# Gated delta attention on one core: the gate's projection is copied to SBUF, and the orders on ScalarE and VectorE change

## The reference, cut to what matters

```python
x = x + 0.5 * ffn(layernorm(x))
x = x + attention(layernorm(x))        # this part
...
# attention, for every head; chunks of 64 rows in the reference
q, k = l2norm(x @ Wq) / 4, l2norm(x @ Wk)
v, gate = x @ Wv, x @ Wg
P = strict_lower(k_beta @ k.T * L)
Ainv = (I + P) * (I + P^2) * (I + P^4) ...
v, k_cumdecay = Ainv @ (v * beta), Ainv @ (k_beta * exp(g))
# scan over the chunks with a state S per head
v_new = v - k_cumdecay @ S
o = q * exp(g) @ S + tril(q @ k.T * L) @ v_new
S = S * exp(g_last) + (k * exp(g_last - g)).T @ v_new
o = rmsnorm(o) * norm_w
o = o * silu(gate)                     # gate * sigmoid(gate)
x = x + o @ Wo
```

## Time and profile before

| what | value |
|---|---|
| median of 3 executions | 1187.23 us (1185.53 to 1190.21) |
| the profiled execution's own time | 1186.16 us |
| its span, first to last instruction | 1184.0 us |
| VectorE busy over the span | 927.2 us, 78% |
| TensorE matmuls busy over the span | 1005.2 us, 85% |
| ScalarE, GpSimd busy over the span | 604.0 us (51%), 408.4 us (34%) |
| mean granted TensorE clock | 0.942 of full speed |

### The profile page before, as it was taken

How to read it: one execution, slowest core, us unless ns; L and a number is a source line. 1 busy time by engine, 2 the same in 40 slices (tenths; PEclk the granted TensorE clock), 3 DMA queues, 4 the chain that set the end, 5 groups by cost and what they waited for, 6 DMA issues and landing times. The chain is left out here.

```text
span 1184.0 us, 38519 instructions
## 1 busy us (share of the span) xinstructions
PE 1005.2 (85%) x15510; PEld 721.5 (61%) x15510; DVE 927.2 (78%) x2432; ACT 604.0 (51%) x1614; POOL 408.4 (34%) x580
## 2 busy tenths in 40 slices
PE   2999977686898989989888887679999896799967
PEld 1888873354555555555565556558888774255546
DVE  3777646349999999999999999527776456899976
ACT  2433326444677777777777775654333262201144
POOL 2667540301221222222222221216665458500047
PEclk9999999788899999999999988879999888899989
DMA  9100005244544445444455543200000023945003
GB/s 251 32 2 1 1 1 174 55 89 100 110 97 107 105 94 110 103 84 105 105 111 111 111 93 76 44 2 1 2 1 1 11 65 87 282 116 170 1 19 125
DMA packets 282626, 93.31 MB, mean 79 GB/s; under 512 B 208977, under 2 KB 275409, under 8 KB 282449
## 3 DMA queue, kind: packets, MB, share of 16 engines
q1 hardware_dynamic: 247056, 84.03, 29.6%
q10 hardware_dynamic: 35392, 6.82, 3.0%
HBM read 56.20 MB, written 30.41 MB: 73 GB/s over the span
## 5 line engine op out<-in xcount | busy, mean ns | idle before, releaser
L1770 DVE TENSOR_TENSOR delta_tmp<-delta_PR 128x130 f32<-128x130 f32 (+12 forms) x416 | 156.4, 376 | 8.9
L1767 DVE TENSOR_TENSOR delta_PR<-delta_PR,delta_tmp 128x130 f32<-128x130 f32 (+12 forms) x416 | 152.5, 367 | 9.3
L1882 POOL TENSOR_TENSOR delta_S<-delta_E,delta_Bm 128x128 f32<-128x128 f32 x32 | 16.9, 527 | 265.3 <-issue 227.4
L1620 ACT ACTIVATE delta_y<-psum 32x128 f32<-32x128 f32 x256 | 68.7, 268 | 60.4 <-PE psum L1455 57.8
L506 POOL TENSOR_TENSOR ffn_H<-ffn_hid,ffn_H 128x512 fp32r<-128x512 f32 x48 | 61.8, 1293 | 57.0 <-DVE ffn_H L472 57.0
L506 POOL TENSOR_TENSOR first_H<-first_hid,first_H 128x512 fp32r<-128x512 f32 x48 | 61.7, 1290 | 52.9 <-DVE first_H L472 52.9
L1636 ACT ACTIVATE delta_wide<-delta_S 32x128 f32<-32x128 f32 x256 | 78.2, 306 | 3.2
L1405 PE MATMUL psum<-delta_MV,delta_KT 32*32 32x128 f32 x2048 | 66.2, 280 | 10.9 <-ACT delta_E L1570 10.9
L438 ACT ACTIVATE first_silu<-psum 128x512 f32<-128x512 f32 x48 | 28.8, 599 | 83.3 <-PE psum L391 83.3
L1421 PE MATMUL psum<-delta_T,delta_pad 128*32 128x128 f32 x2048 | 70.4, 295 | 0.9 <-issue 0.9
L1858 POOL TENSOR_TENSOR delta_VK<-delta_QK,both_eg 128x256 f32<-128x256 f32 x32 | 20.9, 655 | 145.4 <-DVE delta_QK L1703 145.3
(11 more groups left out here) (278 smaller groups left out, 2541.7 us busy)
## 6 DMA issues: line engine op xcount, KB each, us to landing
within_scratch<-delta_PT SPq DMA_DIRECT2D x128, 64.0 KB, 2.0
delta_PR<-within_scratch SPq DMA_DIRECT2D x16, 512.0 KB, 3.8
inverse_scratch<-delta_PR SPq DMA_DIRECT2D x16, 512.0 KB, 3.1
space_T<-taps_scratch SPq DMA_DIRECT2D x8, 1024.0 KB, 5.9
X<-taps_scratch SPq DMA_DIRECT2D x8, 1024.0 KB, 9.0
X<-in_x SPq DMA_DIRECT2D x32, 128.0 KB, 10.1
turned_scratch<-gates_XT SPq DMA_DIRECT2D x16, 256.0 KB, 2.3
delta_xT<-turned_scratch SPq DMA_DIRECT2D x32, 128.0 KB, 2.9
```

Source lines behind the costliest of these rows:

```text
L1620: i = a.activation(dst, heads(bank[6][rows, half * P:(half + 1) * P]), ACT.Copy)
L1767: i = v.tensor_tensor(after, after, t3, ALU.add)
L1770: i = v.tensor_tensor(t3, column.to_broadcast([P, j, n_after]), row.to_broadcast([P, j, n_after]), ALU.mult)
```

## The change

There are four edits, all in the delta phase.

1. A new SBUF tile `raw_gate`. ScalarE's new step `keep_g` does the first exp of the sigmoid and then copies the gate's projection from PSUM to `raw_gate`; before the copy it waits for `keep_gate` of the tile before (`p_gate`), which reads the same buffer.
2. `p_v` is now signalled by that copy, not by `keep_v`. TensorE's `outputs` waits for `p_v` where it waited for `p_gate`, and so does `project_vg` in the first tiles.
3. On ScalarE the second `widen` stands between `keep_g` and the rest of the sigmoid (ln, exp).
4. On VectorE `keep_gate` reads `raw_gate` in place of PSUM and stands behind turn 17 of the solver, not behind turn 12.

```diff
+    M.raw_gate = take("raw_g", DM)
...
         elif t > 0:
-            pe.wait_ge(S.p_gate, t)
+            pe.wait_ge(S.p_v, t)
...
     def outputs(t):
         if t + LAG_SCAN < NT:
-            pe.wait_ge(S.p_gate, t + LAG_SCAN + 1)
+            pe.wait_ge(S.p_v, t + LAG_SCAN + 1)
...
-        a.activation(of_heads(M.VK[t % 6], 0), heads(bank[5][:, 0:DM]), ACT.Copy).then_inc(S.p_v, 1)
+        a.activation(of_heads(M.VK[t % 6], 0), heads(bank[5][:, 0:DM]), ACT.Copy)
...
-    def sigmoid_g(t):
+    def keep_g(t):
         gate = M.gate[t % 9]
         a.wait_ge(S.p_vg, t + 1)
         if t >= 9:
             a.wait_ge(S.o_gate, t - 8)
         own.seq(a.activation(gate, bank[5][:, DM:], ACT.Exp, scale=-1.0))
+        if t > 0:
+            a.wait_ge(S.p_gate, t)
+        a.activation(M.raw_gate, bank[5][:, DM:], ACT.Copy).then_inc(S.p_v, 1)
+
+    def sigmoid_g(t):
+        gate = M.gate[t % 9]
         own.seq(a.activation(gate, gate, ACT.Ln, bias=1.0))
         a.activation(gate, gate, ACT.Exp, scale=-1.0).then_inc(S.p_sig, 1)
...
         at(keep_v, n)
+        at(keep_g, n)
+        at(widen, Z, 1)
         at(sigmoid_g, n)
-        at(widen, Z, 1)
         at(exp_decays, n - LAG_FORM)
...
-        v.tensor_tensor(gate, gate, bank[5][:, DM:], ALU.mult).then_inc(S.p_gate, 1)
+        v.tensor_tensor(gate, gate, M.raw_gate, ALU.mult).then_inc(S.p_gate, 1)
...
-        solve(n, 12, 13)
+        solve(n, 12, 18)
         at(keep_gate, n)
-        solve(n, 13, 21)
+        solve(n, 18, 21)
```

## The result

The changed kernel takes 1192.13 us (median of 15; 1187.83 to 1199.4), the kernel before 1187.05 (15; 1183.97 to 1194.98). The ratio is 1.004, 95% interval 1.0022 to 1.0058: slower by 0.4%, which is within the 0.5% that the prediction called no change, though the interval lies above 1 as a whole. The forecast was 1188.5, so the range held the time and the middle was low by 3.6.

The account below looks back on a forecast made before the run. The prediction took VectorE's instructions to bound the delta phase from 285 to 753 us. Its terms, -2.8 + 2.7 + 0.3 + 0.8 + 0.3 = +1.3 us, on 1187.23 gave 1188.5 us, range 1184.0 to 1193.0.

Parts of the forecast that it names:

- two rivals: Delta phase: turn blocked for its whole fading overlap, 1191.7, 10 in 100; `outputs` not brought forward, 1191.3, 8 in 100.
- the 30.4 us: TensorE's `outputs` waiting for `keep_gate`, 21 times mid-phase; a rival put it on the path, about 1157; 7 in 100, about 1178.
- First term, -2.8: `outputs` starts 1.6 us earlier, so VectorE's 5 waits for TensorE, at `own_heads`, all go: -2.8 us.
- Second term, the displaced turn: A solver turn takes `keep_gate`'s old place beside GpSimd's fading and slows by 0.10, 27 times: +2.7 us.
- Third, the product: `keep_gate` on VectorE with two SBUF sources takes 0.42 and not 0.41: 32 x 0.01 = +0.3 us.
- Fourth, the start: In slots 1 to 3 `exp_decays` stands behind the copy as well: 3 x 0.28 = +0.8 us.
- Fifth, +0.3: Slots 7, 9 and 13, where ScalarE is late: `within` begins 0.1 later behind `exp_decays`: +0.3 us.
- The second rival: The displaced turn beside GpSimd's fading is blocked for all 0.22 us of overlap, 27 times: 5.9 us, 1191.7; 10 in 100.

Follow-up runs that it names:

- e3_fill: Changed kernel plus one extra 128x512 matmul in each of slots 7 to 31, ahead of the second `from_values`; 1189.06 us.
- e5_both: Changed kernel plus that extra matmul, and with `faded_q`, a product reading PSUM, moved from behind turn 5 to behind turn 12 of the solver; 1185.04 us.
- e7_fill_before: Kernel before the change plus the same extra matmul ahead of the second `from_values`; 1190.13 us, ratio 1.0026 to before.
- e2_copy: Kernel before plus ScalarE's copy, with `keep_gate` reading `raw_gate` at its old place and `outputs` still waiting for it; 1196.37 us, ratio 1.0084.
- e1_early: Changed kernel with `keep_gate` back behind turn 12 and the second `widen` back behind the whole sigmoid; copy and its signal stay; 1196.24 us.

## Why the prediction was right, and where it wasn't

Right in its verdict and range (no change by the bound of 0.5%, 1184 to 1193, measured 1192.1); its own sum was +1.3 and the measured difference is 5.1, by the ratio 4.7. That the range held is in part luck: its upper end stood at 1193.0 for two rivals that didn't come, and what raised the time, the clock, is in none of its terms.

- *VectorE is the bound, and the 30.4 us aren't worth their size*: right. The wait is gone and nothing of that order came back.
- *First term, -2.8*: this is the step that failed. The mechanism was right: `outputs` earlier, `own_heads` fed in time, shown by e3_fill, in which all waits are gone and the five slots are 0.56 shorter even with the turn's +0.09 in them. What failed is the sentence that the 1.6 us of idle time move to `from_values` "and the end doesn't see them". A part moved there, 1.03 us became 1.90 and in the later half 0.37 became 1.25 (8.6 us in all became 19.2, where 30.4 were to move), and the clock fell in 10 stretches and not 3. With the falls, the waits are 3.8 us, not 0. What the falls cost, 386.7 - 381.8 = 4.9 us in the 24 slots (4.0 by the second trace), is more than the whole error there: the terms gave these slots -2.8 + 2.4 + 0.2 + 0.3 = +0.1, and they took +3.5. The rest went the other way: e3_fill, nearly without falls, has -1.4, in part since each of the five slots gained 0.65 and not 0.55 and the fifth term cost nothing. The prediction says nothing of the clock, though it stands in the earlier trace rows.
- *Second term, the displaced turn*: 0.10 a slot forecast, 0.09 measured in the turns (0.48 and 0.35), 2.2 to 3.1 us over the 24 slots between kernels with and without it, where 2.4 was said. Right.
- *Third, the product*: +0.01 each, measured 0.42 against 0.41. Right at its new place. What the prediction did not say is that the same product would have cost 0.62 at the old one.
- *Fourth, the start*: 0.28 a slot forecast, 0.27 in slot 1. Right. The sum over slots 0 to 4 can't be tested by it: 36.9 before, 36.2 and 37.5 in two traces of the changed kernel, since the clock falls there too.
- *Fifth, +0.3*: TensorE waits 17 times, 3.5 us in all, for `exp_decays` in the changed kernel, more often than in the three slots named, but VectorE has no wait at `keep_within` over 0.2 us in slots 7 to 31. It costs nothing by itself.
- The second rival gave 1191.7, near the measured time, and for the wrong reason: it wanted turns blocked for the whole overlap, 0.22, and they lost 0.09. That its number fits is chance.

**What stays open.** The 24 slots account for 3.5 us (2.6 in the second trace) of the 5.1 or 4.7 measured. In the profiled executions, the phases behind the delta phase, which are the same in all kernels, took 400.9 us from the last `own_heads` before, 403.7 and 403.3 in the changed kernel, and between 400.7 (e3_fill) and 406.5 (e5_both) elsewhere, with the clock's falls there of different lengths. So one trace can't settle a difference of 1 to 3 us in the whole span, and the rest of the measured slowdown, like the 3.7 us of e7_fill_before, isn't explained. How TensorE's clock is decided is not shown here either, nor whether the matmul of 1.02 us helps by cutting the idle stretch or by the work that it adds; only that filling the idle stretch ahead of `from_values` removes the falls, that a short filling removes half of them, and that moving idle time to that place brings them with no work added or taken (e2_copy and e1_early).

## What to carry to other kernels

A wait removed from an engine that isn't the bound still moves that engine's idle time. Ask where it gathers, and what the clock did at that place before: here the gap ahead of `outputs` went, the one ahead of `from_values` grew by 0.9 us, TensorE's clock fell there, and what the earlier start had gained on VectorE was lost with it; one spare matmul in the gap brought it back. Don't judge by the length of a gap alone, since longer ones stood ahead of `outputs` without a fall. When an instruction leaves its place, price what takes that place by what runs beside it on the other engine, since the same product took 0.41, 0.62 or 0.42 us by its sources and its neighbour.

## What the runs showed of the hardware that was not expected

- The TensorE clock fell to half 10, 9, 11 and 10 times in 24 slots where TensorE idled 1.7 to 2.05 us (later 0.8 to 1.3) ahead of the second `from_values`, and 3, 4, 1 or 0 times where it idled 1.0 to 1.2 (later 0.4) or less there. With a fall, `project_vg` took 3.78 us in place of 1.98.
- Idle pieces of 1.3 to 1.9 us ahead of `outputs`, in the kernel before and in e7_fill_before, had no fall beside them.
- A product of 128x256 on VectorE beside GpSimd's fading took 0.62 us with both sources in SBUF and 0.41 with one in PSUM; alone it took 0.42.
- Adding 25 matmuls to the changed kernel took 4.9 us off the 24 slots (386.7 to 381.8) and 3 off the median (1192.13 to 1189.06).
